# Order of the work on TensorE, VectorE and ScalarE in the middle and at the end of a batch step

## The reference

```python
# per head: S = 256, DH = 64
log_D = fg_mat + ig.T                              # fg_mat from the cumulative sum of log_sigmoid(fg)
max_log_D = jnp.max(log_D, axis=-1, keepdims=True)
D = jnp.exp(log_D - max_log_D)
C = (q @ (k.T / sqrt(DH))) * D
normalizer = jnp.maximum(jnp.abs(C.sum(-1, keepdims=True)), jnp.exp(-max_log_D))
h = C / (normalizer + EPS) @ v                     # then an RMS norm of each head
...
def bitlinear(x, w):                               # 8-bit activations by token, ternary weights
    return act_quant(x) @ weight_quant(w).T
h = jnp.square(jax.nn.relu(bitlinear(x, w_gate))) * bitlinear(x, w_up)
ffn = bitlinear(h, w_down)
...
x = x + jnp.tanh(g_xattn[0]) * xattn(layernorm(x), ctx, ctx, ...)
x = x + jnp.tanh(g_ffn[0]) * ffn(layernorm(x))
```

## Time and profile before

| | before |
|---|---|
| median of 3 runs | 637.5 us (636.77 to 637.85) |
| profiled execution, its own time | 638.38 us |
| its span, first to last instruction | 636.7 us |
| TensorE busy | 578.6 us, 91% of the span |
| VectorE busy | 526.7 us, 83% |
| ScalarE busy | 454.3 us, 71% |
| GpSimd busy | 129.9 us, 20% |
| mean granted TensorE clock | 0.965 |
| longest chain by engine | PE 59%, DVE 17%, issue 10%, ACT 6%, DMA 5% |

### The profile page before, as it was taken

How to read it: one execution, slowest core, us unless ns; L and a number is a source line. 1 busy time by engine, 2 the same in 40 slices (tenths; PEclk the granted TensorE clock), 3 DMA queues, 4 the chain that set the end, 5 groups by cost and what they waited for, 6 DMA issues and landing times.

```text
span 636.7 us, 18420 instructions
## 1 busy us (share of the span) xinstructions
PE 578.6 (91%) x6596; PEld 338.0 (53%) x6596; DVE 526.7 (83%) x1144; ACT 454.3 (71%) x925; POOL 129.9 (20%) x266
## 2 busy tenths in 40 slices
PE   7592768999999999999999999999999999999896
PEld 4361443656555564656555565646565555656442
DVE  4479595898989989898989899898989899897964
ACT  5374979858685877858686868768586868677662
POOL 1256240212121202112121202021121212021200
PEclk9785968999999999999999999999999999999998
DMA  9884505041140505050320505050412305020000
GB/s 311 306 287 139 192 2 167 18 140 62 43 159 17 182 0 199 0 182 17 103 95 19 179 8 191 0 187 11 156 43 77 121 17 183 3 100 1 34 19 33
DMA packets 45169, 63.73 MB, mean 100 GB/s; under 512 B 1872, under 2 KB 26704, under 8 KB 45136
## 3 DMA queue, kind: packets, MB, share of 16 engines
q1 hardware_dynamic: 45136, 63.30, 28.8%
HBM read 54.77 MB, written 8.52 MB: 99 GB/s over the span
## 4 chain that ended last, share of the span: by engine, by line
PE 59%; DVE 17%; issue 10%; ACT 6%; DMA 5%; DVEq 1%; POOL 1%; SPq 0%; ACTq 0%; POOLq 0%
PE ub L1090 15%; PE gb L1090 14%; PE yb L1116 10%; PE ab L1124 6%; PE tp L1137 5%; PE ab L1104 3%; DVE ssq L883 3%; DMA stage<-in_w_up 2%; PE ab L1125 2%; DVE stage L805 2%; DMA xs<-in_x 2%; DVE stage L755 1%; DMA max_rows<-mrow 1%; PE ab L1198 1%; DVE dmat L862 1%
## 5 line engine op out<-in xcount | busy, mean ns | idle before, releaser
L1090 PE MATMUL ub<-wuT,xqT 128*128 128x512 bf16 x512 | 133.1, 383 | 2.0 <-DVE stage L755 2.0
L1090 PE MATMUL gb<-wgT,xqT 128*128 128x512 bf16 x512 | 133.3, 383 | 1.5 <-ACT xqT L551 1.5
L524 ACT ACTIVATE relu<-gb 128x512 f32<-128x512 f32 x128 | 75.4, 589 | 77.3 <-PE gb L1090 75.1
L1116 PE MATMUL yb<-wdT,stage 128*128 128x512 bf16 x512 | 122.8, 384 | 3.6 <-ACT stage L538 3.6
L755 DVE TENSOR_TENSOR stage<-relu,ub 128x512 f32<-128x512 f32 x128 | 87.0, 680 | 26.6 <-ACT relu L526 26.1
L862 DVE SCALAR_TENSOR_TENSOR dmat<-ab,dmat 128x384 f32<-128x384 f32 x128 | 65.3, 551 | 31.7 <-POOL dmat L429 22.7
L526 ACT ACTIVATE relu<-relu 128x512 f32<-128x512 f32 x128 | 80.7, 631 | 4.1
L1090 PEld LDWEIGHTS ub<-wuT,xqT 128*128 128x128 bf16 x512 | 50.3, 99 | 61.2 <-DVE stage L755 3.0
L1116 PEld LDWEIGHTS yb<-wdT,stage 128*128 128x128 bf16 x512 | 47.4, 99 | 53.4 <-issue 4.7
L1090 PEld LDWEIGHTS gb<-wgT,xqT 128*128 128x128 bf16 x512 | 46.0, 100 | 49.9 <-ACT xqT L551 1.8
L429 POOL TENSOR_SCALAR_AFFINE_SELECT dmat<-dmat 128x256 f32<-128x256 f32 x128 | 55.3, 461 | 68.0 <-ACT dmat L570 67.9
(11 more groups left out here) (110 smaller groups left out, 870.8 us busy)
## 6 DMA issues: line engine op xcount, KB each, us to landing
dmat<-max_rows SPq DMA_DIRECT2D x16, 1024.0 KB, 5.1
values<-in_ctx_v SPq DMA_DIRECT2D x16, 520.0 KB, 7.7
xs<-in_x SPq DMA_DIRECT2D x16, 512.0 KB, 5.9
cT<-in_ctx_t SPq DMA_DIRECT2D x16, 512.0 KB, 6.9
out<-stage SPq DMA_DIRECT2D x32, 256.0 KB, 2.0
stage<-in_w_gate SPq DMA_DIRECT2D x4, 1024.0 KB, 12.7
stage<-in_w_up SPq DMA_DIRECT2D x4, 1024.0 KB, 11.1
stage<-in_w_down SPq DMA_DIRECT2D x4, 1024.0 KB, 5.6
```

The costliest lines, as they stand in the source:

```text
L524: nc.scalar.activation(relu[:, c % 2, :], gb[c % 2][:, :], ACT.Relu).then_inc(g_free, 1)
L1090: last = nc.tensor.matmul(bank[c % 2][:, :], xqT[par][:, t, d, :], w[:, d, c * CH:(c + 1) * CH], start=(d == 0), stop=(d == KD - 1))
L1116: done = nc.tensor.matmul(yb[:, :], hqT[:, c, :], wdT[:, c, :], start=(c == 0), stop=(c == KF - 1))
```

## The change

Only the order within the `step` functions changes; no instruction is added or taken away. On TensorE: `hidden_transposes(b - 1, 1)` goes ahead of the third pair's `heads_out(n, 2)`; `q_columns(m)` goes between `heads_out(n, 2)` and `heads_out(n, 3)`; `a_rows(m)` goes behind both halves of `chunk(b, 1, 0)`; where there is no n (the last step), `down(b, 0)` goes in one piece behind `chunk(b, 1, 3)`. On ScalarE `hidden_cols(b - 1, 1)` goes ahead of `heads(n, 2)`. On VectorE `cumulative(m)` goes ahead of `output(b - 1, 1)`; where there is no m, `hidden(b, 1, 0)` goes ahead of `token_stats`; in the last step `output(b, 0)` goes behind `quantise_low(b, 1)`.

```diff
@@ ScalarE step @@
                 relu_square(b, 0, 3)
-                if n is not None:
-                    heads(n, 2)
                 if prev:
                     hidden_cols(b - 1, 1)
                 if n is not None:
+                    heads(n, 2)
                     heads(n, 3)
                     squares(n)
@@ VectorE step @@
                     scale_heads(n)
+                if m is not None:
+                    cumulative(m, par)
                 if prev:
                     output(b - 1, 1, npar)
-                if m is not None:
-                    cumulative(m, par)
                 if n is not None:
                     residual(n, npar)
                 if m is not None:
                     running_max(m, par)
+                else:
+                    hidden(b, 1, 0)
                 if n is not None:
                     token_stats(n, npar)
-                hidden(b, 1, 0)
+                if m is not None:
+                    hidden(b, 1, 0)
@@
                 hidden_max(b, 1, 1)
-                output(b, 0, par)
+                if n is not None:
+                    output(b, 0, par)
                 hidden_scale(b, 1, par)
                 quantise_low(b, 1)
+                if n is None:
+                    output(b, 0, par)
@@ TensorE step @@
                 chunk(b, 0, 3, par)
-                if n is not None:
-                    heads_out(n, 2, npar)
                 if prev:
                     hidden_transposes(b - 1, 1)
                 else:
                     weight_total(2)
                 if n is not None:
+                    heads_out(n, 2, npar)
+                if m is not None:
+                    q_columns(m, par)
+                if n is not None:
                     heads_out(n, 3, npar)
-                if m is not None:
-                    q_columns(m, par)
                 if prev:
                     down(b - 1, 1, 0, KF // 2)
@@
-                chunk(b, 1, 0, par, 0, 1)
+                chunk(b, 1, 0, par)
                 if m is not None:
                     a_rows(m, par)
-                chunk(b, 1, 0, par, 1, 2)
                 chunk(b, 1, 1, par)
@@
-                down(b, 0, 0, KF // 2)
-                chunk(b, 1, 3, par)
-                if n is not None:
+                if n is not None:
+                    down(b, 0, 0, KF // 2)
+                    chunk(b, 1, 3, par)
                     token_columns(n)
-                down(b, 0, KF // 2, KF)
+                    down(b, 0, KF // 2, KF)
+                else:
+                    chunk(b, 1, 3, par)
+                    down(b, 0, 0, KF)
```

More of the change, by code:

```diff
@@ L1269, in step @@
                 if n is not None:
-                    heads_out(n, 3, npar)
+                    heads_out(n, 2, npar)
                 if m is not None:
                     q_columns(m, par)
+                if n is not None:
+                    heads_out(n, 3, npar)
                 if prev:
```

## The result

The changed kernel takes 643.68 us (median of 4 runs, 643.1 to 645.29), the kernel before beside it 637.15 us: ratio 1.0105, 95% interval 1.0084 to 1.0126. It is slower by about 1%, which is small but clear of the noise. The profiled execution took 645.29 us, the longest of the four; its span is 643.6 us against 636.7.

What follows compares the result with a forecast made beforehand. TensorE was taken to set the pace, with VectorE close behind. Steps 1 to 13 +7.9, step 0 +2.2, step 14 -0.1 and the end -2.7 sum to +7.3 on 637.5: 644.8 us, range 639.8 to 647.3 (8 in 10).

Steps and rivals of the forecast that it cites:

- The stall for a goes: TensorE, transposes of a: moved behind the whole chunk they no longer wait for VectorE, -0.97 us a step.
- q's second tile is gated by L796: TensorE, q's transposes: the second tile can't start before VectorE's copy ends, leaving 1.2 us of idle TensorE.
- Rival B: q's transposes: no gate there, the step gains about 0.4 us, 631.8 us in all; chance 0.05.
- The tile switch behind q costs 0.10: TensorE, between q and the fourth pair: changing from full array to 128x64 tiles costs 0.10 us.
- L870 starts 1.61 us later and the delay goes through whole: VectorE, from L870 to tile 1's first L755: one unbroken sequence passes on the whole 1.61 us delay.
- Rivals A and D: A: VectorE's lag is absorbed, 634.5 us, chance 0.08. D: nothing measurable, step +0.2 at most, 637.5 us, chance 0.05.
- The up half's wait for L755 sets the step: TensorE, chunk 2's up half: waits about 0.3 us for VectorE's product, so a step grows by 0.61 us.
- Rival C: Steps: VectorE's lag passes in part, TensorE's own path (+0.3) sets the step, 640.8 us or 639.2; chance 0.14.
- The 0.16 from output and GpSimd: VectorE's second L915: later output delays GpSimd's residual, and VectorE inherits about 0.16 us.
- Step 0, +2.2: First step: third pair behind the weight total, then q and fourth pair at half clock, +2.2 us.
- Step 14, -0.1: Step 14: the up half's stall goes but down still waits for L538; a saved tile switch leaves -0.1 us.
- The end, -2.7: Last step: last transposes 1.72 us earlier and 1.0 us no longer lost to a halved clock, -2.7 us.

Runs made afterwards that it cites:

- e1: The whole change without the swap (q's transposes stay behind the fourth pair, third pair ahead of the hidden transposes), against the kernel before: 621.28 us, ratio 0.974.
- e6: e1 with output kept ahead of cumulative on VectorE: 624.35 us, ratio 0.9795 against the kernel before.
- e4: The whole change plus, on VectorE, the copy hidden_cols ahead of the three-chunk maximum and the fourth chunk's product: 636.2 us, ratio 0.9984 against the kernel before.
- e7: e1 with the copy of the turned activations ahead of the fourth chunk's product on VectorE: 624.4 us.
- e2: The kernel before with only the swap around the last two pairs of heads on TensorE and ScalarE: 660.25 us, ratio 1.0347.
- e5: The whole change, but steps 0 and 14 keep the old order around the last two pairs of heads on TensorE and ScalarE: 641.46 us.
- e3: The kernel before with only the last step's edits, down in one piece behind the last chunk and output behind quantising: 634.60 us, ratio 0.995.

## Why the prediction was right, step by step

Forecast 644.8 us, measured 643.68; a rise of 7.3 us forecast, 6.5 measured. The mechanism held: the stall for a goes, q's second tile is gated, and VectorE's lag costs more than the stall gave. That the total came out so near is in part luck. The main term, the steps, was 1.9 us too large, and three pieces that were too small or not forecast (step 0, step 14, the start) made up for 1.4 us of it.

- **The stall for a goes.** Right: of 12.1 us 0.2 are left, and e1 shows its worth, 1.06 us of a steady step (35.22 to 34.16), 0.97 forecast. e6 shows that cumulative ahead of output was needed for 0.2 us of it.
- **q's second tile is gated by L796.** Right: in after it goes on 0.14 us behind the copy, in 13 steps; e4, which moves only the copy, sets it free. Rival B is refuted.
- **The tile switch behind q costs 0.10.** Right: from q's second half to the fourth pair 0.56 us (379.24 to 379.80), against 0.46 to 0.49 to `down`; in e4 eight transposes take 1.02 us ahead of the pair, in e7 0.93 ahead of `down`. The reading that it was free would have been wrong.
- **L870 starts 1.61 us later and the delay goes through whole.** Right: +1.65, and 9.83 against 9.82 us from there to L755. e2 shows the same delay, unabsorbed, at a. Rivals A and D are refuted by e1 and e2 together.
- **The up half's wait for L755 sets the step, by about 0.3 us over TensorE's own path.** Right in kind, wrong in size: L754 does end last in the steps of after, but by 0.10 to 0.18 us. TensorE's own path grew by about 0.4 us and not by 0.28, since the late copies of q and the late logarithm cost it 0.5 us and not 0.3, while the stall gave back 1.08 and not 0.97. Rival C, in which that path alone sets the step, is closer to what happened than its price says: with 0.4 us a step and C's own other terms it would have come to 642 us (an estimate from these rows), inside the stated range.
- **The 0.16 from output and GpSimd.** Wrong in size: 0. Output's end did move by 1.84 us in the step, but GpSimd's residual took 1.64 us on average instead of 1.77, and VectorE's statistics are in their old place behind L869 (+1.66 against +1.65). The product ends last, so these 0.11 us are missing from the step: a steady one grew by 0.5 us (35.22 to 35.75) and not by 0.61. In the sum of steps 1 to 13 it is 6.0 and not 6.9, since before held 0.7 us of issue gap in step 2 that after did not show; no run tells why.
- **Step 0, +2.2.** Right: 2.5 in the profiled pair, 2.9 in e5. Third pair, q and fourth pair start at 81.51, 83.01 and 84.91, 1.50 and 1.90 us apart as worked out, at half clock.
- **Step 14, -0.1.** Wrong in sign: +0.5. I let the fourth pair follow the third 0.85 us later and did not ask for the bank: ScalarE must first copy tp, so 1.48 us.
- **The end, -2.7.** Right in number: -2.6, with the clock at full, and e3 alone gives it. The reason given for 1.0 us of it does not hold as a rule: e2 idles 2.21 us at the same place and keeps its full clock. The 1.6 us of order would have come in any case, the 1.0 only where the clock falls in before.

Term by term, forecast and profiled: steps 1 to 13 7.9 and 6.0, step 0 2.2 and 2.5, step 14 -0.1 and 0.5, the end -2.7 and -2.6, the start 0 and 0.5; in all 7.3 and 6.9.

## What to carry to other kernels

Before moving an instruction ahead on an in-order engine, find its own gate in the trace: a group that takes longer from start to start than its parts (1.22 us where 0.92 would do) is already waiting, even where no wait is named, and what stood ahead of it was its cover; whatever is moved behind it inherits the whole wait. When two engines are both nearly full, price a delay where the second engine's unbroken sequence starts and look for the place where the first meets its end; a gain and a loss in the same step are best tested apart, since here one change held a gain of 16 us and a loss of 22. Where one stall is filled by moving a neighbour, look at what that neighbour was covering. And where two paths end within a few tenths of a microsecond of each other, as TensorE's and VectorE's do at the third chunk, forecast both, and expect little from speeding up one of them alone.

## What the runs showed of the hardware

An operation on VectorE that reads the tile which the one directly ahead of it writes starts about 0.2 us later than with another operation between them (0.81 us from product to maximum in e4 against 0.60 from product to the next independent operation), and nothing in the waits view names it. VectorE shows the same gap in before (390.95 to 391.76), where product and maximum stand side by side in tile 1.

An idle piece of about 2 us in TensorE's work does not decide by itself what happens to its clock. Full clock was kept through 1.82 us (step 14 of before), 1.90 us (step 14 of after), 2.12 us (e4), 2.21 us (the end of e2) and 2.40 us (step 0 of after, ahead of 105.10), and fell to 0.50 after 2.12 us (e7, the same place as in e4) and 2.22 us (the end of before, the same place and order as in e2). The fall cost 1.7 us behind e7's idle piece and 1.0 us at the end of before. What decides is not shown by any run here, so a forecast that counts on the fall, or on its absence, is a guess about one execution.
